# Overflow slots of a mixture of experts in blocks of 64, two experts to a block, on the column halves of TensorE

## The reference

```python
scores = x @ gate_w.T                        # 1024 tokens, 8 experts
mult, sel = _masked_sampling_omp(scores)     # two experts per token
h = silu(einsum('th,efh->etf', x, w1)) * einsum('th,efh->etf', x, w3)   # H 256, F 512
y = einsum('etf,ehf->eth', h, w2)
coef = (one_hot(sel, 8) * mult[..., None]).sum(axis=1)
out = einsum('te,eth->th', coef, y)
```

## Time and profile before

| | us |
|---|---|
| median of 3 runs | 232.21 |
| lowest, highest | 231.79, 232.42 |
| the profiled execution | 231.6 |
| its span, first to last instruction | 229.87 (printed as 229.9) |
| PE busy in the span | 212.2 |
| DVE, ACT, POOL busy | 125.9, 87.1, 86.6 |

### The profile page before, as it was taken

The page is one execution under the profiler, slowest core; times in us unless marked ns, Lnnn a source line. Parts: engine busy times, 40 slices in busy tenths (PEclk is TensorE's granted clock), DMA queues, the critical chain, the costliest instruction groups (busy, mean ns, idle before and its releaser), DMA issues.

```text
span 229.9 us, 3859 instructions
## 1 busy us (share of the span) xinstructions
PE 212.2 (92%) x1272; PEld 165.2 (72%) x1273; DVE 125.9 (55%) x445; ACT 87.1 (38%) x193; POOL 86.6 (38%) x112
## 2 busy tenths in 40 slices
PE   8999989999999989989899999999999999999810
PEld 7796743356864467889799899999999976666510
DVE  3796897999979789978874957211111111111100
ACT  2866655984005460333612722222222223232300
POOL 8347229210011200537323344444763234455540
PEclk9999999999999999999999999999999999999985
DMA  6867044089992157162502313232312311221000
GB/s 178 223 219 233 29 156 157 23 324 414 411 408 89 54 193 304 47 224 86 166 14 29 43 22 62 46 48 38 57 48 26 43 22 22 27 26 10 4 7 3
DMA packets 17049, 26.04 MB, mean 113 GB/s; under 512 B 4350, under 2 KB 12677, under 8 KB 17030
## 3 DMA queue, kind: packets, MB, share of 16 engines
q1 hardware_dynamic: 11328, 20.14, 24.6%
q0 software_dynamic: 4320, 5.25, 13.0%
q10 hardware_dynamic: 1382, 0.41, 0.9%
HBM read 21.34 MB, written 5.77 MB: 118 GB/s over the span
## 4 chain that ended last, share of the span: by engine, by line
PE 51%; DVE 28%; ACT 6%; issue 5%; POOL 2%; DMA 2%; DVEq 1%; POOLq 0%; ACTq 0%
PE PS L1974 20%; PE PS L1998 10%; PE PS L2004 7%; PE PS L1675 3%; PE PS L2018 3%; DVE stat L1001 3%; DVE hT L1393 3%; ACT a L790 2%; PE PS L1960 2%; PE PS L1739 2%; DVE work L1079 1%; DVE x L1253 1%; DMA out_dram<-a,sidx 1%; DVE mv L1008 1%; DVE work L1065 1%
## 5 line engine op out<-in xcount | busy, mean ns | idle before, releaser
L1974 PE MATMUL PS<-hT,e 128*128 128x128 f32 x480 | 58.9, 276 | 1.1 <-ACT hT L914 0.6
L1974 PEld LDWEIGHTS PS<-hT,e 128*128 128x128 f32 x480 | 56.8, 192 | 2.5 <-ACT hT L914 1.2
L1641 DVE TENSOR_TENSOR hT<-th,PS 128x512 f32<-128x512 f32 x20 | 13.7, 686 | 63.6 <-PE PS L1974 38.1
L1857 PE MATMUL PS<-xnT,e 128*128 128x512 f32 x88 | 39.6, 598 | 2.0 <-DVE hT L1393 0.9
L1857 PEld LDWEIGHTS PS<-xnT,e 128*128 128x128 f32 x88 | 16.1, 190 | 22.2 <-issue 17.4
L1998 PE MATMUL PS<-e,hT 128*128 128x256 f32 x120 | 28.6, 381 | 0.2 <-DVE x L1431 0.2
L1998 PEld LDWEIGHTS PS<-e,hT 128*128 128x128 f32 x120 | 21.7, 190 | 3.2 <-issue 0.8
L604 POOL TENSOR_TENSOR rstd<-veps,nhalf 128x2 f32<-128x2 f32 x12 | 8.7, 728 | 39.1 <-DVE veps L1010 39.1
L665 POOL DMA_INDIRECT out_dram<-a,ids_early x8 | 12.8, 1596 | 26.5 <-ACT a L943 14.5
L1871 PE MATMUL PS<-e,hT 128*128 128x256 f32 x96 | 21.7, 383 | 0.0
L924 ACT ACTIVATE th<-PS 128x512 f32<-128x512 f32 x20 | 11.9, 594 | 22.5 <-PE PS L1974 15.2
(11 more groups left out here) (276 smaller groups left out, 331.7 us busy)
## 6 DMA issues: line engine op xcount, KB each, us to landing
e<-e_in SPq DMA_DIRECT2D x24, 512.0 KB, 8.2
x<-x_in SPq DMA_DIRECT2D x2, 512.0 KB, 6.2
graph_rows<-e SPq DMA_DIRECT2D x4, 256.0 KB, 2.4
out_dram<-x SPq DMA_DIRECT2D x4, 256.0 KB, 2.5
xn_rows<-xn SPq DMA_DIRECT2D x4, 256.0 KB, 2.4
e<-gw_in SPq DMA_DIRECT2D x1, 768.0 KB
e<-uw_in SPq DMA_DIRECT2D x1, 640.0 KB
e<-dw_in SPq DMA_DIRECT2D x1, 640.0 KB
```

The costliest lines, as they stand in the source:

```text
L1641: dve.tensor_tensor(hh[me], th[:, me, :], PS[:, 2 + me, :], ALU.mult).then_inc(gated, 1)
L1857: mm = pe.matmul(PS[:, bank, :], w[:, k, it * P:(it + 1) * P], xnT[:, h, k, :], start=(k == 0), stop=(k == 1))
L1974: mm = pe.matmul(PS[:, bank + q, f * P:(f + 1) * P], w[:, k * F + f * P:k * F + (f + 1) * P], xgT[q][:, k, :], start=(k == 0), stop=(k == 1))
```

## The change

Overflow is cut into halves of 64 slots instead of blocks of 128 (`HALF`, `iota_h`: thresholds 128, 192, 256, ...). Two halves, in general of two experts, make one pack: slots 0 to 63 and 64 to 127 of one gathered block. Two packs (blocks 16 and 17, `PACKS`) are written out behind all sixteen first blocks, so block 15 becomes an ordinary first block and `STATIC` is 18. Further packs, if the data ask for them, go through a loop behind.

- In a pack each product is made for its two halves: 64 columns of tokens, stationary, give 64 partitions of the result, and each half streams the weights of its own expert (`up_pack`, `down_pack`).
- Which experts the halves belong to is known at run time alone. SP therefore loads their weights again from HBM, by a register from `eoff`, into the places of experts whose late block is over (`staged_in`, `freed_by`, `stage`): twelve loads of 512 KB for the two packs, behind blocks 8 to 11.
- A token can be in both halves of a pack, with two experts. One scatter must not add twice to one row, so a 128 x 128 matrix of equal rows (`same`) adds the two results: `spread_rows` on PE and `same_rows` on DVE make it, `merge` multiplies the scaled result by it, `copy_merged` takes it out, and `pack_ids` leaves the second of two equal rows out of the scatter.
- Gathers 14 to 17 and all scatters get places in `POOL_ORDER`.

```diff
-STATIC = 2 * E - 1
-OVER = 14
-NO = OVER + 2
+PACKS = (E + 8, E + 9)
+STATIC = 2 * E + len(PACKS)
+HALF = P // 2
+NH = 24
+NO = NH // 2
 NL = E + NO
+MOST = 6 * 2
...
+        pack_row = sb("pack_row", [P, 2])
+        pack_ids = sb("pack_ids", [P, 2], U32)
+        twice = sb("twice", [P, 2])
+        same = [work[:, p, :] for p in range(2)]
+        raw = [z[0][:, p * C:(p + 1) * C] for p in range(2)]
...
-                     ("gate", 5), ("shares", 1), ("gate", 6), ("coefs", 1)]
+                     ("gate", 5), ("shares", 1), ("gate", 6), ("coefs", 1), ("gate", 7), ("same", 0)]
...
-                      ("gather", 13), ("gather", 14)]
+                      ("gather", 13), ("scatter", 9), ("gather", 14), ("scatter", 10), ("gather", 15), ("scatter", 11),
+                      ("gather", 16), ("scatter", 12), ("gather", 17), ("scatter", 13), ("scatter", 14), ("scatter", 15),
+                      ("scatter", 16), ("scatter", 17)]
...
+            return [slice(e * 1024, (e + 1) * 1024) for e in (LATE[2 * p], LATE[2 * p + 1])]
...
+            return [E + 2 * p, E + 2 * p + 1]
...
+            sp.wait_ge(eoff_ready, 1)
+            for p in range(len(PACKS)):
+                for n in range(2):
+                    cols, free, row = staged_in(p)[n], freed_by(p)[n], row_of(slice(2 * p + n, 2 * p + n + 1))
+                    sp.wait_ge(up1_done, free + 1)
+                    stage(e1, e1_in, cols, row, staged[p])
+                    sp.wait_ge(up3_done, free + 1)
+                    stage(e3, e3_in, cols, row, staged[p])
+                    sp.wait_ge(y_done, free + 1)
+                    stage(e2, e2_in, cols, row, staged[p])
...
+            for j in range(7, STATIC + 2):
+                if j < STATIC:
+                    silu(j)
+                if j - 1 in PACKS:
+                    copy_hhT(PACKS.index(j - 1), (j - 1) % 2)
+                if j - 2 in PACKS:
+                    copy_merged(PACKS.index(j - 2))
+                if j + 1 < STATIC:
+                    copy_x(j + 1)
+                if j <= STATIC:
+                    scale_y(j - 1)
...
+                dve.tensor_scalar(eoff[:, :], eblk[:, :], float(E - 1), float(P), ALU.min, ALU.mult).then_inc(eoff_ready, 1)
+                own(dve.tensor_scalar(blocks[:, 0:1], incl[:, E - 1:E], 1.0, -1.0, ALU.max, ALU.add))
+                dve.tensor_scalar(blocks[:, 1:2], blocks[:, 0:1], 2, None, ALU.logical_shift_right).then_inc(blocks_ready, 1)
+
+            def same_rows(h):
+
+                dve.wait_ge(list_ready, 2)
+                for p in range(len(PACKS)):
+                    ins = dve.tensor_scalar(same[p][:, 0:P], ident[:, :], pack_row[:, p:p + 1], None, ALU.mult)
+                ins.then_inc(row_numbers, 1)
+                for p in range(len(PACKS)):
+                    dve.wait_ge(rows_spread, 1)
+                    n = mark(dve.tensor_scalar(same[p][:, P:2 * P], PS[:, 7, p * P:(p + 1) * P], pack_row[:, p:p + 1], None, ALU.is_equal))
+                after(n)
+                for p in range(len(PACKS)):
+                    n = mark(dve.tensor_reduce(twice[:, p:p + 1], same[p][:, P:P + HALF], AX.X, ALU.max))
+                after(n)
+                own(dve.tensor_scalar(twice[:, :], twice[:, :], later_half[:, 0:1], None, ALU.mult))
+                dve.tensor_tensor(pack_ids[:, :], pack_row[:, :], twice[:, :], ALU.add).then_inc(same_ready, 1)
...
+            def up_pack(w, bank, q, p, ready):
+
+                a, b = staged_in(p)
                 for k in range(2):
-                    mm = pe.matmul(PS[:, bank + q, :], xgT[q][:, k, :], w[:, bass.ds(at + k * F, F)],
-                                   start=(k == 0), stop=(k == 1))
+                    for n, cols in enumerate((a, b)):
+                        half_of = slice(n * HALF, (n + 1) * HALF)
+                        mm = pe.matmul(PS[half_of, bank + q, :], xgT[q][:, k, half_of], w[:, cols][:, k * F:(k + 1) * F],
+                                       start=(k == 0), stop=(k == 1))
                 mm.then_inc(ready, 1)
...
+            def spread_rows(h):
+
+                pe.wait_ge(row_numbers, 1)
+                for p in range(len(PACKS)):
+                    mm = pe.matmul(PS[:, 7, p * P:(p + 1) * P], ones[:, :], same[p][:, 0:P], start=True, stop=True)
+                mm.then_inc(rows_spread, 1)
+
+            def merge(p):
+
+                pe.wait_ge(y_scaled, PACKS[p] + 1)
+                pe.wait_ge(same_ready, 1)
+                pe.matmul(PS[:, 7, p * C:(p + 1) * C], same[p][:, P:2 * P], raw[p], start=True, stop=True).then_inc(merge_done, 1)
...
-            for j in range(7, STATIC):
-                up1(j)
+            for j in range(7, STATIC + 2):
+                if j in PACKS:
+                    p = PACKS.index(j)
+                    pe.wait_ge(xgT_copied, j + 1)
+                    pe.wait_ge(gated, j - 1)
+                    pe.wait_ge(staged[p], 16 * 6)
+                    up_pack(e1, 0, j % 2, p, up1_done)
+                elif j < STATIC:
+                    up1(j)
                 if j == 7:
                     block_list(3)
-                turn_x(j + 1)
-                up3(j)
-                down(j - 1)
...
+                if j == 9:
+                    spread_rows(0)
+                if j - 1 in PACKS:
+                    if j - 1 == PACKS[0]:
+                        pe.wait_ge(coef_ready, 2)
+                    turn_h(j - 1, (j - 1) % 2)
+                if j - 2 in PACKS:
+                    merge(PACKS.index(j - 2))
+                if j + 1 < STATIC:
+                    turn_x(j + 1)
+                if j in PACKS:
+                    up_pack(e3, 2, j % 2, p, up3_done)
+                elif j < STATIC:
+                    up3(j)
+                if j - 1 in PACKS:
+                    down_pack(j - 1, PACKS.index(j - 1), (j - 1) % 2, PACKS.index(j - 1))
+                elif j <= STATIC:
+                    down(j - 1)
```

More of the change, by code:

```diff
@@ L356, in build @@
         gidx_set = sem("gidx_set")
+        row_numbers = sem("row_numbers")
+        rows_spread = sem("rows_spread")
+        same_ready = sem("same_ready")
+        staged = [sem(f"staged{p}") for p in range(2)]
+        staged_more = [sem(f"staged_more{p}") for p in range(2)]
+        gathered_more = sem("gathered_more")
+        merge_done = sem("merge_done")
+        merged = sem("merged")
         gathered = [sem(f"gathered{s}") for s in range(E)]
@@ L545, in _, with row_of, stage @@
                 sp.wait_ge(rows_stored[p], 16)
+            def row_of(half):
+                return sp.value_load(eoff[0:1, half], min_val=0, max_val=(E - 1) * P)
+            def stage(w, src, cols, row, signal):
+                sp.dma_start(w[:, cols], src.rearrange("e p n -> (e p) n")[bass.ds(row, P), :]).then_inc(signal, 16)
+            sp.wait_ge(eoff_ready, 1)
[8 more added lines that the diff above has]
+                    stage(e2, e2_in, cols, row, staged[p])
+            pairs = pairs_in_use(sp)
+            with sp.Fori(0, pairs) as i:
+                for q in range(2):
+                    v = i * 2 + q
+                    sp.wait_ge(y_done, v + (STATIC - 1))
+                    for n in range(2):
+                        row = row_of(bass.ds(v * 2 + (4 + n), 1))
+                        for w, src in ((e1, e1_in), (e3, e3_in), (e2, e2_in)):
+                            stage(w, src, staged_in(q)[n], row, staged_more[q])
         @block.gpsimd
@@ L1658, in _ @@
                 search(FILL.get(stage, 0))
-            for j in range(7, STATIC + 1):
+            for j in range(8, STATIC):
                 gate(j)
@@ L1954, in _ @@
             W2 = [e2[:, e * 1024:(e + 1) * 1024] for e in range(E)]
-            def turn_x_over(j, q, s, gathers):
-                pe.wait_ge(gathered[s], gathers)
-                for k in range(2):
-                    mm = pe.transpose(PS[:, 4, q * 256 + k * P:q * 256 + (k + 1) * P], xg[s][:, k * P:(k + 1) * P],
-                                      ident[:, :])
-                mm.then_inc(xgT_done, 1)
             def turn_x(j):
@@ L1968, in turn_x @@
                     pe.wait_ge(xgT_copied, j)
[L1969 removed]
+                pe.wait_ge(gathered[j % E], 16 * (j // E + 1))
+                for k in range(2):
+                    mm = pe.transpose(PS[:, 4, (j % 2) * 256 + k * P:(j % 2) * 256 + (k + 1) * P], xg[j % E][:, k * P:(k + 1) * P],
+                                      ident[:, :])
+                mm.then_inc(xgT_done, 1)
             def up(w, bank, q, ready):
```

216 lines of the change are left out of this document (105 added, 111 removed).

## The result

The changed kernel takes 273.54 us (four runs, 272.25 to 274.51), the kernel before 232.31 us beside it; the ratio is 1.177, interval 1.171 to 1.183. The forecast was 223.6 us, faster. The profiled execution took 273.24 us.

A forecast was written before the change was run, and what follows sets the result against it. TensorE's unbroken chain was taken as the bound, followed by an uncovered tail. T at 193.5 + 12.4 = 205.9 us plus the tail gave a span of 221.25 us, 8.6 less; forecast 223.6 us, range 221.8 to 227.0.

The forecast's parts named there:

- T: End of pack 16's down product on TensorE, forecast at 193.5 + 12.4 = 205.9 us; the tail is counted from it.
- the loop as a rival: Loop over further packs: a fifth half makes it run, two packs with six loads each, none overlapped, 245 us; chance 0.02.
- `spread_rows`: Two f32 products of 128 columns, four passes, added inside TensorE's full stretch with nothing to hide them: +0.45 us.
- gate 8: Queued on DVE behind `same_rows`, which waits for the `spread_rows` product; forecast to start by 158.1 us and take 0.69 us.
- the end of block 14's down product: On TensorE, just before the packs' stretch: 192.84 + 0.13 + 0.45 + 0.1 = 193.5 us.
- The stall at gate 8: Block 8's down product on TensorE waits for the delayed gate: 0.1 us (0 to 0.3).
- Full overlap of the halves: Packs' half products run two at a time: up product 1.72 us, down 1.73; without overlap 3.44 and 3.46.
- The change of array mode: TensorE going between whole and half array: 0.2 us a change, seven before T, 1.4 us.
- The tail: Scatter 16 starts at T + 2.8, lands after 3.4 us; scatter 17 at T + 7.0; end 8.15 + 0.2 us later.
- The reloads: SyncE's twelve 512 KB weight loads between blocks 8 and 11, there by 185 us, cover 15 us: hidden, zero cost.
- the rival "crowding": Reloading crowds queues; gathers or scatters take twice 3.6 to 3.8 us, four 1 us waits, blocks 9 to 12: 227.6 us; chance 0.04.
- Gather 14: Queued behind scatter 9, at about 168.3 us, its transpose at 178 us: no wait, zero cost.

The follow-up runs named there:

- the branch: The changed kernel with each engine's loop over further packs inside a branch taken only if the number of pairs is not zero: 223.06 us, ratio 0.960 to the kernel before.
- with two together: Branch, gathers 14 to 17 and equal rows earlier, plus the packs' up products in pairs: 221.77 us, against 222.10 us for the kernel without the pairing.

## Why the prediction was wrong

**The step that failed** is one sentence: "The number of pairs in the new loop is (4 - 1) >> 2 = 0, so the loop that stages more weights doesn't run." The count was right, the DMA records and the branch both confirm it, and the "so" was wrong: the body runs once at a count of 0, which put 51 us behind T that the sum had at nothing. The profile of before couldn't show it: there the count is (4 + 1) >> 1 = 2 (lines 1635 and 1636). I had the loop as a rival, at 0.02, but with a fifth half as the cause, and the count spoke against that; that the loop might run on nothing wasn't among the cases.

**The price of that rival** was off too: 245 us, two packs at 8.2 us of loading each batch. A pass through the loop costs 51 us of the span, counted from T (50.5 us between the medians): its loads hold up scatter 17, which starts at T + 10.33 us and with the branch at T + 7.06 (3.3 us), and from that scatter to the end it is 271.2 - 216.09 = 55.1 us, with the branch 221.8 - 214.44 = 7.4 us (47.7 us). Loads are 6.9 us of it, and the serial ring, which I hadn't worked out, the rest.

**With the loop out of the way** the sum of the prediction can be read against the kernel with the branch, 223.06 us to the forecast 223.6:

- `spread_rows` 0.46 us (forecast 0.45), gate 8 at 157.84 us (158.1), the end of block 14's down product 193.68 us (193.5), all three in the changed kernel, which is the same up to there.
- The stall at gate 8 was mis-sized. Block 8's down product should have been done at 155.80 + 0.46 + 0.22 + 1.79 + 1.73 = 160.00 us, and is at 158.58 + 1.99 = 160.57: 0.57 us, where I had 0.1 (0 to 0.3). It starts 0.31 us late, at 158.58 instead of 158.27 us, and then takes 1.99 instead of 1.73 us, which I had left out.
- Full overlap of the halves, right. The record of one up product's passes (ns lowest/median/highest, first and last start):

```profile
L2086 PE MATMUL PS<-e,hT x8: 592/592/643, 193.6 to 195.0; 128*64 128x512 f32 x8
```

  Eight passes of 512 columns start within 1.4 us, and the starts come in pairs 7 ns apart (193.614 and 193.621, 194.094 and 194.101). In the earlier trace rows four full ones take 1.72 us. Product against product it is 1.87 for 3.44 us with the way in, 3.58 for 6.88 with two together. The estimate from the Trainium skill, TensorE: Matmul & The Clock Gate, Part 3 (1.59 for two column tiles, from its 2.38 for three) doesn't agree: it would have made 2.16 us of the up product. The measurement decides; three column tiles, for which the page has its figure, were not run here.
- The change of array mode: into a half product 0.15 us (1.87 for 1.72), into transposes 0.15 us (0.37 for 0.22, 0.59 for 0.44), into a down product 0.19 us (1.92 for 1.73). Seven are 1.1 us where I had 1.4. The Trainium skill, TensorEngine Tiling (Array Packing), Key Properties, that a change of mode drains the engine, agrees; the trace gives it a size.
- T at 205.76 us (205.9), which is closer than the terms were. The stall took 0.47 us more than forecast, the changes 0.3 us less, and the changed kernel's execution was already 0.33 us ahead where TensorE's list is still that of before (a down product that starts at 147.10 us in the kernel before starts at 146.77 here). The three cancel nearly. With the branch T was 207.38 us. Of these 1.6 us, 1.02 were there at that same down product (147.79 us; the cause is open), 0.12 came at gate 8, and 0.5 at the gather.
- The tail: scatter 16 starts at T + 2.5 us (2.8) and lands after 3.70 us (3.4) with 69 rows in it, scatter 17 starts at T + 7.06 us (7.0), and the end comes 7.4 us behind (8.35, taken from the earlier trace rows). Of that 1 us, 0.57 is GpSimd's last instruction of any length, a drain behind the last landing: 4.24 us in the kernel before, 3.67 us here. With T 1.5 us late and the end 1 us early the span is 221.8 us (221.25), and the profiled execution took 223.68 us (223.0). That the median of 223.06 us lies below the forecast of 223.6 is luck: I added 0.6 us for a median above the profiled execution, and here it lies 0.6 us below.
- The reloads, forecast at nothing: 0.960 against 0.959, nothing. Scatters took 8.6 us instead of 3.7 to land beside them, over twice their time, which is the threshold that the rival "crowding" named. Gather 14, forecast at about 168.3 us, came at 171.80 us in the changed kernel and at 173.35 with the branch; one wait of 0.5 to 0.9 us came of it in two of the profiled executions with reloads, not the four of 1 us.

## What to carry over

A hardware loop with a count from the data, written as here, has to be read as "at least once" until a trace with the count 0 says otherwise; before relying on 0, put a branch around it, or look for what used to keep the count above 0. When a dynamic tail is replaced by static code, price the dynamic code as if it ran once on nothing, and price it as the chain of its waits, not as its transfers. And when column halves are used, order the work by array mode.

## What was not expected of the hardware

- A scatter that skips all of its 128 rows still takes 2.70 to 2.75 us to land, with 69 rows 3.6 to 3.7 us: about three quarters of it is there without any row.
- Half-array matmuls of different columns overlap also when the program has four passes of one half ahead of the other's (1.87 us), and in part when it has eight (2.63 for 1.73 us): here a pass could start beside the one four ahead of it, and no earlier.
- A change between whole and half array costs 0.15 to 0.19 us.
- TensorE's granted clock changed between its two levels (2.4 and 1.2 GHz) during the ring, so that the 0.72 to 0.75 of the windows above are means. It was 1.00 up to 212.33 us; TensorE had been busy for 55.38 of 55.70 us up to T and for 3.92 of 6.56 us from there. It was 0.50 from there to 229.39 us (busy for 4.46 of 17.06 us), also through 3.78 us of up products without a gap, and then 1.00 again; it changed three times more before the end.
- GpSimd's drain behind the last scatter takes 3.7 to 4.2 us of the span.
